# Three attention loops of a Trainium2 kernel: TensorE turns a tile's shares three rounds behind its scores instead of two

## What is computed

```python
x = x + _L1_xattn_ref(ctx_1024, _layernorm(x), ctx_1024, ..., 8)        # l1
    dot1 = softmax(einsum('blk,bmk->blm', Qs, Ks)) * 0.5
    dot2 = softmax(einsum('blk,bmk->blm', Vs, Ks)) * 0.5
    out  = einsum('blm,bmk->blk', dot1, K) + einsum('blm,bmk->blk', dot2, K)
    ...
x = x + _L2_xattn_ref(_layernorm(x), ctx_1024, ctx_1024, mask, ...)     # l2
    energy = where(mask == 0, -1e20, einsum('nhqd,nhkd->nhqk', q, k))
    out = einsum('nhqk,nhkd->nhqd', softmax(energy / sqrt(DH)), v)
    ...
x = x + _L3_xattn_ref(_layernorm(x), ctx_1024, ctx_1024, ...)           # l3
    out = einsum('bhqk,bhkd->bhqd', softmax(scores / sqrt(dk)), V)
    ...
```

## Time and profile before

| | |
|---|---|
| median of 3 runs | 1018.8 us (1018.56 to 1018.99) |
| the profiled execution, its own time | 1018.33 us |
| its span, first to last instruction | 1016.5 us |
| PE busy | 839.3 us, 83% of the span |
| DVE busy | 752.0 us, 74% |
| ACT busy | 569.8 us, 56% |
| POOL busy | 437.2 us, 43% |
| loop of l1 | from 193 to 282 us |
| loop of l2 | from 434 to 515 us |
| loop of l3 | from 907 to 986 us |

### The profile page before, as it was taken

One profiled execution on the slowest core, in us unless ns is written; L12 is line 12 of the kernel. 1 busy time (PEld: TensorE's weight loads), 2 busy tenths in 40 slices (PEclk: granted clock), 3 DMA queues, 4 the chain that ended last, 5 costly groups with the idle time before them and its releaser, 6 DMA issues. The chain is left out here.

```text
span 1016.5 us, 28652 instructions
## 1 busy us (share of the span) xinstructions
PE 839.3 (83%) x11477; PEld 632.0 (62%) x11477; DVE 752.0 (74%) x1825; ACT 569.8 (56%) x1316; POOL 437.2 (43%) x286
## 2 busy tenths in 40 slices
PE   4275699779828999679876999999999998977888
PEld 3153545778616777534554878787787877744457
DVE  4989786778764554678879678685867768789974
ACT  3172244457714554357776674847567483347774
POOL 5000130498216776288501462634335263619810
PEclk9588799799958999799998999999999999999999
DMA  5422000300061112300010001010001100000001
GB/s 163 114 61 84 1 1 1 142 32 2 2 231 46 53 51 47 89 1 2 2 53 1 3 28 29 3 28 3 28 5 28 29 3 3 3 2 1 2 2 42
DMA packets 27135, 36.09 MB, mean 35 GB/s; under 512 B 7835, under 2 KB 20444, under 8 KB 26238
## 3 DMA queue, kind: packets, MB, share of 16 engines
q1 hardware_dynamic: 21310, 27.84, 8.7%
q0 software_dynamic: 2496, 5.12, 1.9%
q10 hardware_dynamic: 3200, 1.31, 0.5%
HBM read 26.98 MB, written 7.27 MB: 34 GB/s over the span
## 5 line engine op out<-in xcount | busy, mean ns | idle before, releaser
L2129 DVE TENSOR_TENSOR soft_outs<-soft_expert_ps,soft_bias 128x512 f32<-128x512 f32 x128 | 87.1, 688 | 75.2 <-PE soft_expert_ps L1847 73.5
L1847 PE MATMUL soft_expert_ps<-soft_W,soft_slots 128*32 128x128 f32 x4096 | 125.7, 275 | 2.4 <-DVE soft_outs L2129 2.4
L1847 PEld LDWEIGHTS soft_expert_ps<-soft_W,soft_slots 128*32 128x32 f32 x4096 | 109.2, 110 | 21.0 <-issue 21.0
L953 POOL TENSOR_TENSOR l_prob<-l_prob,l_inv 128x1024 f32<-128x1024 f32 x48 | 91.3, 1902 | 40.4 <-DVE l_inv L1107 40.0
L1939 ACT ACTIVATE soft_slots<-soft_slot_ps 128x512 f32<-128x512 f32 x128 | 69.4, 598 | 64.1 <-PE soft_slot_ps L1833 64.1
L2024 POOL TENSOR_TENSOR l_ring<-l_ring,soft_inv 128x1024 f32<-128x1024 f32 x15 | 35.1, 2372 | 104.7 <-DVE soft_inv L2122 54.6
L1092 DVE TENSOR_REDUCE l_under<-l_score 128x16 f32<-128x1024 f32 x48 | 58.6, 1222 | 27.3 <-PE l_score L1173 14.6
L1794 PE MATMUL soft_slot_ps<-phi,xnT 128*128 128x256 f32 x256 | 68.9, 406 | 9.6 <-ACT soft_spread L1927 6.4
L982 PE MATMUL l_turned<-ident,l_prob 128*128 128x128 f32 x384 | 52.5, 280 | 22.8 <-POOL l_prob L953 22.8
L1861 PE MATMUL soft_mix_ps<-soft_outs,soft_combT 128*32 128x128 f32 x2048 | 68.8, 275 | 2.1 <-DVE soft_acc L2145 2.1
L1056 ACT ACTIVATE l_probT<-l_turned 128x512 f32<-128x512 f32 x96 | 52.1, 594 | 32.7 <-PE l_turned L982 32.7
(11 more groups left out here) (450 smaller groups left out, 2180.4 us busy)
## 6 DMA issues: line engine op xcount, KB each, us to landing
moe_w<-in_moe_W SPq DMA_DIRECT2D x2, 2048.0 KB, 10.1
soft_W<-in_soft_W SPq DMA_DIRECT2D x16, 256.0 KB, 3.0
kept<-early SPq DMA_DIRECT2D x1, 2048.0 KB, 6.3
l_keys<-in_moe_b SPq DMA_DIRECT2D x1, 2048.0 KB, 8.6
l_asked<-kept SPq DMA_DIRECT2D x1, 2048.0 KB, 13.3
ctxT<-in_ctxT SPq DMA_DIRECT2D x1, 1024.0 KB, 5.1
moe_rows<-xn_tok SPq DMA_DIRECT2D x4, 256.0 KB, 3.7
expert_rings<-moe_back SPq DMA_DIRECT2D x4, 256.0 KB, 5.5
```

Source lines behind the costliest of these rows:

```text
L953: nc.gpsimd.tensor_tensor(prob[t % 4][:], prob[t % 4][:], inv[t % 2][:].unsqueeze(2).broadcast_to(S16), ALU.mult).then_inc(share_done, 1)
L1847: last = nc.tensor.matmul(expert_ps[c][32 * j:32 * j + 32, h, tt, :], slots[u % 3][:, h, tt, 128 * c + 32 * j:128 * c + 32 * j + 32], W[i ...
L2129: nc.vector.tensor_tensor(outs[u % 3][:, c].rearrange("p h t d -> p (h t) d"), expert_ps[c][:].rearrange("p h t d -> p (h t) d"), bias[i % ...
```

## The change

`turn` and `take_turned` are called one round later. `mix_tile` and everything else stay in their rounds.

```diff
@@ PE's stream
                     mix_tile(i - 4)
                 if i in (2, 3):
                     keep_busy(nc, core, spare, 8)
-                if there(i - 2):
-                    turn(i - 2, 0, turned_a, probT_a)
-                    turn(i - 2, 1, turned_b, probT_b)
+                if there(i - 3):
+                    turn(i - 3, 0, turned_a, probT_a)
+                    turn(i - 3, 1, turned_b, probT_b)
@@ ACT's stream
                     take_mix(i - 4)
                 if i == T + 1:
                     norm.deviate(act, 0)
-                if there(i - 2):
-                    take_turned(i - 2, 0, turned_a, probT_a)
-                    take_turned(i - 2, 1, turned_b, probT_b)
+                if there(i - 3):
+                    take_turned(i - 3, 0, turned_a, probT_a)
+                    take_turned(i - 3, 1, turned_b, probT_b)
                 if there(i):
                     exponentiate(i)
```

## The result

The median of 4 runs is 1006.1 us (1004.93 to 1007.67), against 1018.9 us (1018.56 to 1018.99) before: a ratio of 0.987, 95% interval 0.9858 to 0.9883. The forecast was 1006.7 us, its range 1003.5 to 1010.5. The profiled execution took 1005.51 us, with a span of 1003.7 us, 12.8 less than before.

The account below looks back on a forecast made before the run. PE's waits for POOL's share, a cycle over two rounds, were taken to bound the loops. Gains of 4.95, 4.05 and 3.05 us off 1018.33 gave 1006.3, the median 0.5 above: 1006.7 us, range 1003.5 to 1010.5.

Parts of the forecast that it names:

- The limit of before: All three loops: a two-round cycle through POOL's share, with PE idle 22.8 us ahead of its transposes.
- The three next limits: Steady rounds after: PE's own 4.13 us in l1, put_out's wait for the add 3.97 in l2, DVE's 3.72 in l3.
- cycle over `out`: One buffer: put_out waits for the previous tile's add; 7.93 us per two rounds, 3.97 a round in l2.
- The rival in which `put_out` takes over the whole wait: l2 and l3 keep steady rounds of 4.18 and 3.92 us, only their starts gain; 1009.9 us, chance 0.08.
- the drain gave back: Loop ends lose part of the gain: 0.75 us in l1, 0.45 each in l2 and l3, bounds 0 and 1.5.
- the part of it that I added for the norm: In the drains, 0.2 us more in the norm that follows, within the 0.45 taken back in l2 and l3.
- The slower rival: Every round's mix waits for ACT's late copies, 0.9, 0.4, 0.2 us in l3, l2, l1; 1031 us, chance 0.03.
- The sum: Loop gains of 4.95 in l1, 4.05 in l2 and 3.05 in l3: 12.05 us.
- The half-rate stretch: A 6 us stretch at clock 0.72 costs 2 to 3 us: one more 1009.5, one fewer 1004; chance 0.11.

Follow-up runs that it names:

- early add: Changed kernel with DVE's add moved from the end of its round to between the shift and the sums: 1000.5 us median, ratio to before 0.9812.
- late mask: Changed kernel with POOL's mask work moved from rounds 1 to 4 of l1 to rounds 13 to 16: 1006.62 us; with DVE's add also moved, 999.0 us.
- run with late copies: Changed kernel with ACT's copies of the turned shares put behind the round's exponentials, not ahead of them: 1017.68 us.
- old order with the early add: Kernel before, turns two rounds behind, with DVE's add moved ahead of the row sums in every round: 1027.71 us against 1019.4 us.

## Why the prediction was right

**The limit of before.** Confirmed from two sides: moving the turn and halving the share give the same rounds.

**The three next limits.** Forecast 4.13 / 3.97 / 3.72 us a round, measured 4.13 / 3.97 / 3.71. In l2 the rounds alternate between 3.90 and 4.03, as the text said, and `put_out`'s wait in l3 is the forecast's 0.3. The early add confirms the cycle over `out` in l2: without it the round falls to 3.80, while those of l1 and l3 stay at 4.13 and within 0.03 of 3.71. That PE's work bounds l1 and DVE's l3 is read from the windows (32.00 of 32.00 and 39.24 of 40.00 us), not tested by making that work shorter. The rival in which `put_out` takes over the whole wait is out.

**l1.** The scores of tile 7 were to start near 220.1 and did at 220.70, in a loop that began 0.6 later. Those of tile 15 start at 253.76, where 253.2 and that 0.6 give 253.8. PE and POOL there:

```profile
219.77 1.09 PE L982 MATMUL l_turned<-ident,l_prob 128*128 128x128 f32 x8 [0.77 <-POOL l_prob L953]
220.70 1.50 PE L1173 MATMUL l_score<-xnT,l_asked 128*128 128x128 f32 x12
...
253.76 1.95 PE L1173 MATMUL l_score<-xnT,l_asked 128*128 128x128 f32 x16
```

POOL's shares 4.97 us apart set this start, as the forecast had it; the late mask shows it by its absence. The last exponentials start at 258.63, against 263.76 before, which with that 0.6 is 5.7 us earlier in the loop, as forecast. The stage gained 5.0, so the drain gave back 0.7, forecast 0.75.

**l2 and l3.** 4.5 and 3.5 us against 4.05 and 3.05. The mechanism held and the terms were a little off. The row maximum of tile 7 gained 3.1 and 2.2 us, forecast 2.9 and 1.9: the first rounds take 3.48 or 3.49 us and not the 3.55 that I took from a steady round less the add's place, since the row maximum takes 1.16 us there and 1.22 later. Then eight rounds bring 1.7 more, as forecast. The drains gave back 0.25 and 0.4 instead of 0.45. The mix that is held for its copies, l2, PE, for the earlier trace rows:

```profile
498.36 0.64 PE L992 MATMUL l_mix<-l_probT,l_keys 128*32 128x128 f32 x16 [0.39 <-issue]
498.94 1.09 PE L982 MATMUL l_turned<-ident,l_prob 128*128 128x128 f32 x8
...
500.81 0.65 PE L992 MATMUL l_mix<-l_probT,l_keys 128*32 128x128 f32 x16
```

and ACT beside it:

```profile
491.17 0.84 ACT L1046 ACTIVATE l_prob<-l_shifted 128x768 f32<-128x768 f32 x1
...
495.33 1.28 ACT L106 ACT_TABLE_LOAD   x1
...
497.19 1.07 ACT L1056 ACTIVATE l_probT<-l_turned 128x512 f32<-128x512 f32 x2
```

From the last exponentials to the last mix it is 9.64 us, against 9.30; from the table load on 5.48, forecast 5.5. The mix of tile 14 stands behind the copies at 497.19. So this give-back is in its place, only the part of it that I added for the norm did not come.

**The slower rival.** The mix doesn't wait in steady rounds. The run with late copies shows that the slack could have been lost, and that the price per round would have been smaller than I put it (0.10 to 0.16 us, not 0.2 to 0.9) but that of the loops' starts larger, by the clock, which the forecast did not have.

**The sum.** The loops gave 13.0 where 12.05 was forecast, and 0.2 of it went between them; the median lies 0.56 above the profiled execution, where 0.5 was taken. So the forecast's error of 0.6 us is the terms of l2 and l3, each 0.45 too small, less those 0.2. That the parts outside the loops would stay within 2 us held, the largest change being 1.5. That they came to 0.2 together is luck: +0.6, +1.1 and -1.5 cancelled, and single runs of the changed kernel lie 2.7 us apart, so the agreement of the whole to 0.6 us says less than that of the rounds.

**The half-rate stretch.** In the profiled execution one is gone, the one behind l2 (below), though the forecast had those behind the loops remain; the part that holds it is the one that took 1.5 us less. The forecast's price of 2 to 3 us doesn't follow from its own figures: 4.80 less 3.5 is 1.3.

## What to carry to other kernels

A software pipeline's round is set by its longest cycle, not by the idle time shown at one wait. Find the next cycle before removing the first, and price only the difference: here 22.8 us of waits were worth 13. An edit's sign depends on which cycle binds: moving one short add made each round 0.10 us longer in the old order and took 5.8 us off the three stages in the new. And look at the first rounds and at the drain apart from the steady ones, since other work (the mask here) may set them.

## What was unexpected on the chip

Behind pauses of 2 to 3.4 us on PE at the start of a loop, with little work around them, the clock was down in the run with late copies and in the old order with the early add: the same turn took 1.97 us in place of 1.09. In the first of them that happened in all three loops. In the kernel before, the same pauses as in the second one left the clock at 1.00, so the length of a pause doesn't decide it alone. Windows of l3 in the run with late copies:

```profile
916.00:919.00 3.00, 0.73 (x8) 0.00 (x0) 2.93 (x5) 1.68 (x6) 3.00 (x2) 0.96 0.00 0
919.00:922.00 3.00, 1.91 (x20) 1.55 (x21) 2.93 (x4) 1.72 (x4) 3.00 (x3) 0.50 0.02 5
922.00:925.00 3.00, 3.00 (x16) 1.06 (x16) 0.18 (x1) 2.14 (x7) 3.00 (x3) 0.50 0.00 0
```

After the fall PE is busy for 3.00 of 3.00 us at 0.50: the half rate lengthens the path itself, and DVE stands idle for it (0.18 of 3.00).

Behind l2 the stretch of 0.72 is gone in the changed kernel, whose next stage begins at 507.51:

```profile
506.00:512.00 6.00, 4.80 (x22) 3.61 (x22) 3.37 (x7) 2.39 (x4) 0.00 (x0) 1.00 0.53 163
```

Over all profiles here the parts outside the loops, which no edit touches, took 192.1 to 194.4, 150.9 to 153.4 and 390.0 to 393.1 us. I take these differences for such stretches that a shift in time meets or misses, but haven't shown it for each. They may be why single runs of one kernel are 2 to 4 us apart. The length of a stage tells more here than the time of a run.
